# In the cross steps, the heads are normalised in front of row maximum 6

## The chip, the core and the metric

The kernel runs on one core of one Trainium2 chip. A core has five engines that run side by side, each through its own instructions in a fixed order: TensorE (PE, with its weight loads listed apart as PEld), VectorE (DVE), ScalarE (ACT), GpSimd (POOL) and SyncE (SP), which here only starts transfers. They wait for one another through semaphores. The metric is the time of one execution in device microseconds, as the median of several runs.

## What is computed

The reference is a decoder of two layers on 16 sequences of 256 tokens and 256 features. Layer 0 is windowed self attention, cross attention to a context of 77 tokens with a padding mask per sequence, and a mixture of 8 experts of which each token takes two. Layer 1 is causal self attention, cross attention with one mask for all sequences, and a quantised gated network. Cut to what matters here:

```python
x = x + window_attention(layernorm(x))            # call 1, items 0 to 15
x = x + cross_attention(layernorm(x), ctx, pad)   # call 1, items 16 to 31
x = x + mixture_of_experts(layernorm(x))
x = x + causal_attention(layernorm(x))            # call 2, items 0 to 15
x = x + cross_attention(layernorm(x), ctx, mask)  # call 2, items 16 to 31
x = x + gated_network(x)
# attention of one sequence, 16 heads of 16 features
scores = q @ k.T / 4 ; p = exp(scores - rowmax(scores)) ; heads = (p @ v) / rowsum(p)
```

## The kernel before

`attention` is called twice, once for each layer. In the trace the tiles of the first call carry the name window, those of the second the name causal, also where they work for the cross attention. A call handles 32 items: item 0 to 15 is the self attention of one sequence each, item 16 to 31 its cross attention. The work of one item is spread over several steps of a software pipeline. In step `ref`, item `ref` has its layernorm turned and its projections made, item `ref - 1` has its scores and row maxima, item `ref - 2` its shifted scores, exponentials and first products with the values, item `ref - 3` the last of these products and its heads, and item `ref - 4` its output projection. `active(ref, lag)` says whether there is such an item. In the last items of a call, statistics for what follows are added (`last_ln`), and in call 1 the choice of experts as well (`find_best` and `choose`, L1114 to L1138, from step 22 on).

Every engine has its own `step`, written out by hand as a loop over eight slots `i`, and this order is all that sets the order of its work. `wide(ref)` is true where the layer of item `ref - 2` handles two pairs of heads at once:

```python
GROUP = {"window": 1, "causal": 1, "cross_pad": 2, "cross_mask": 2}
def wide(ref):
    return active(ref, 2) and layer_at(ref, 2).pairs == 2
```

So the wide steps are the cross steps, 18 to 33 of each call; the others are the self steps.

The parts that the change and the prediction touch, for a wide step:

- TensorE, `wide_slot` (L2073): in slot 6 it makes `scores` 6 (L1685 for the padding, L1692), then `early_maxima` (L1849), then `heads_out` (L2009), which turns the heads of item `ref - 3` into the bank `psb` and raises `o_mm`, then `shifted` 6 (L1721, L1726). In slot 7 it makes `first_quads` (L1746) and then `turn_outputs` (L1831), which waits for `o_norm`. The next step begins with `scores` 0, `turn_normed` (L1831), `shifted` 0, then in slot 1 the first half of the query projection (L1877) and `late_maxima` (L1849), and in slot 2 `scores` 2.
- `scores` writes the two banks of `ps1`, which every call of it uses again, so it waits until VectorE has taken the row maxima before (`s1_max`). In a wide step it is called in slots 0, 2, 4 and 6.
- VectorE, `step` (L1256): `row_max` 6 waits for `scores` 6 and reduces `ps1`. With the padding mask that is one reduction (L1078), with the common mask it is eight masked ones (L1072, each followed by a read of its result). Behind it in slot 6 stands the normalisation of the heads: a wait for `o_mm`, a reciprocal (L1272), a wait for it, two multiplications (L1277), and `o_norm` is raised. Then follow in slots 6 and 7 the statistics of the rows just finished (L75, L80), `split_max` (L1053, L1055), which `late_maxima` waits for, `low_key` (L1036), and in call 1 the choice of experts; then the next step's `row_max` 0, for which `scores` 2 waits. In slot 4 VectorE waits for the output projection (`add_output`, L1090), in slot 5 of call 2 it takes a peak (L1292).
- SP copies queries and keys of item `ref` into `q_pair` and `k_pair` (L615, L622). It takes the keys first, after `k_lo` from `low_key` and after `shifted` 2.
- GpSimd takes the inverse deviation of the last statistics (L53, L55) and sends rows to the experts (L814).

In the self steps the same normalisation stands in slot 6 behind that slot's row maximum too, and a row maximum is taken in every one of the eight slots.

Of the kernel before, what the change touches and what calls it, by code (L numbers as in the profile page):

```python
# [12 lines left out]
ALU = mybir.AluOpType  # L13
# [6 lines left out]
H = 16  # L20
HD = D // H
P = 128
# [61 lines left out]
def normalise(nc, ln, par, rows, out, normed, b):  # L84

    for s in range(ST):
        op = nc.vector.tensor_scalar(out[:, s, :], rows(b, s), ln["mv"][par][:, s, 0:1],
                                     ln["rstd"][par][:, s:s + 1], ALU.subtract, ALU.mult)
    op.then_inc(normed, 1)
# [98 lines left out]
def attention(nc, layers_in, x_sb, q_pair, k_pair, v_aug, ident, selects, to_all, eye, parts, merge=None, tail=None, route=None,  # L188
# [8 lines left out]
    with ExitStack() as ctx:  # L197
        def sb(name, shape, dt):
            return ctx.enter_context(nc.sbuf_tensor(f"{tag}_{name}", shape, dt))
# [21 lines left out]
        recip = sb("recip", [P, ST * H], F32)  # L221
# [132 lines left out]
        o_mm = sem("o_mm")  # L354
        recip_done = sem("recip_done")
        o_norm = sem("o_norm")
# [52 lines left out]
        o_heads = psb[:, :, :].rearrange("p a (h d) -> p (a h) d", d=VW)  # L409
        o_by_half = o_tok[:].rearrange("p s (q a j) d -> p a (s q) j d", a=2, j=2)  # L410
# [44 lines left out]
        def active(ref, lag):  # L455

            return 0 <= ref - lag < N
# [5 lines left out]
        def wide(ref):  # L463

            return active(ref, 2) and layer_at(ref, 2).pairs == 2
# [45 lines left out]
        def layer_at(ref, lag=0):  # L511

            return layers_in[(ref - lag) // B]
# [16 lines left out]
        def in_x(t, ref):  # L530

            r = ref // B
            return lambda i, s: row_of(t - r * B, s)
# [17 lines left out]
        with nc.Block(no_gpsimd_drain=True) as block:  # L551
            @block.sync
            def _(sp):
# [26 lines left out]
                if load:  # L580
                    x_view, _, x_second, x_loaded = load
                    sp.dma_start(x_sb[:, ST:TILES // 4, :], x_view[:, ST:TILES // 4, :]).then_inc(x_second, 16)
# [396 lines left out]
            def _(dve):  # L979
# [78 lines left out]
                def row_max(t, ref, i):  # L1058

                    L = layer_at(ref, 1)  # L1060
                    if i % L.pairs:
                        return
                    hf, j = i // 4, i % 4
                    dve.wait_ge(s1_mm, before(t, ref, 1) + i // L.pairs + 1)
                    if L.mask_nat is not None:
                        gate(dve, dve_passed)
                        junk = 0
                        for p in range(L.pairs):
                            for qt, _, nk, col in L.direct:
                                for ab in range(2):  # L1070
                                    nk_real = min(nk, L.nk)
                                    op = nc.vector.tensor_tensor_reduce(  # L1072
                                        masked[:, junk:junk + nk_real], ps1[:, ab, p * L.width1 + col:p * L.width1 + col + nk_real],
                                        L.mask_nat[0][:, col:col + nk_real], 1.0, LEAST_SCORE, ALU.add, ALU.max,
                                        m_tok[:, hf, ab, j + p, qt:qt + 1])
                                    junk += nk_real
                    else:
                        op = nc.vector.reduce_max(  # L1078
                            m_tok[:, hf, :, j:j + 2, :].rearrange("p a j s -> p a (j s)"),
                            ps1[:, :, 0:2 * L.width1].rearrange("p a (j k) -> p a j k", j=2 * ST)[:, :, :, 0:S2], AX.X)  # L1080
                    op.then_inc(s1_max, 1)
# [165 lines left out]
                def next_rows(t, ref):  # L1247

                    if active(ref, -1):
                        par = (ref + 1) % 2  # L1250
                        dve.wait_ge(scaled_by, t + 2)
                        if ref >= 1:
                            dve.wait_ge(xT_mm, t)
                        normalise(nc, ln, par, in_x(t + 1, ref + 1), xn[par], normed, t + 1)

                def step(t, ref):  # L1256
                    par = ref % 2
                    if ref == B:
# [6 lines left out]
                    for i in range(PAIRS_H):  # L1265
                        if i == 4 and wide(ref):
                            next_rows(t, ref)
                        if active(ref, 1):
                            row_max(t, ref, i)
                        if i == 6 and active(ref, 3):  # L1270
                            dve.wait_ge(o_mm, t - 2)
                            nc.vector.reciprocal(recip[:].unsqueeze(2), o_heads[:, :, HD:HD + 1]).then_inc(recip_done, 1)  # L1272
                            dve.wait_ge(recip_done, t - 2)
                            for ab in range(2):
                                heads = slice(ab * H, ab * H + H)
                                by_quad = lambda x: x.rearrange("p (q j) d -> p q j d", j=2)
                                op = nc.vector.tensor_tensor(o_by_half[:, ab], by_quad(o_heads[:, heads, 0:HD]),  # L1277
                                                             by_quad(recip[:, heads].unsqueeze(2).to_broadcast([P, H, HD])), ALU.mult)
                            op.then_inc(o_norm, 1)
                        if i == (4 if wide(ref) else 1) and active(ref, 4):  # L1280
                            add_output(t, ref, 4)
                        late = bool(merge) and ref == 0
# [5 lines left out]
                        if i == (3 if ref == N + 3 else 5 if wide(ref) else 1) and tail and in_tail(ref, 5):  # L1288
# [3 lines left out]
                            op = nc.vector.tensor_reduce(tail.peak[:, bass.ds(e, 1)], last_xn[0], AX.XY, ALU.max,  # L1292
                                                         apply_absolute_value=True)
# [63 lines left out]
                if not merge:  # L1357
                    scale_layer(0)
                dve.wait_ge(loaded[0], 16 * n_load[0])
                steps(dve, step)  # L1360
                if route:
                    tile_table()
# [1674 lines left out]
```

## Time and profile before

| | |
|---|---|
| median of 3 runs | 2112.07 us (2107.06 to 2112.20) |
| the profiled execution | 2101.48 us, its span 2099.7 us |
| PE, PEld busy in the span | 1948.5 us (93%), 1597.3 us (76%) |
| DVE, ACT, POOL busy | 1233.8 us (59%), 979.4 us (47%), 686.7 us (33%) |
[...]

Times in the rows are microseconds from the start of the span. The trace is of one execution; the time of that execution is given beside its span, since some 1.8 us lie around it.

### The profile page before, as it was taken

How to read it: one execution, taken by the hardware profiler on the slowest of the kernel's cores; microseconds unless marked ns; L12 is line 12 of the kernel's file. 1: busy time of each engine (PE TensorE's matmuls, PEld its weight loads, DVE VectorE, ACT ScalarE, POOL GpSimd, SP SyncE). 2: the span in 40 equal slices, each digit the busy share in tenths (PEclk: the TensorE clock that was granted, in tenths of full speed). 3: DMA queues.
4: the chain of work that ended last, by engine and by line, in shares of the span. 5: the costliest groups of instructions: out<-in, count | busy, mean ns of one | idle time of the engine just before them, and what ended most of it. 6: DMA issues, size and time to landing. Idle time of an engine off the chain costs nothing. (4 is left out here: it accounts for less than half of the span.)

```text
span 2099.7 us, 57083 instructions
## 1 busy us (share of the span) xinstructions
PE 1948.5 (93%) x19802; PEld 1597.3 (76%) x19802; DVE 1233.8 (59%) x5200; ACT 979.4 (47%) x1905; POOL 686.7 (33%) x1244
## 2 busy tenths in 40 slices
PE   7999998999959999999999789999899998999889
PEld 5788886777749999999999578887677775444377
DVE  5788885676541111111115588998778886369964
ACT  2555555676613333333333255556566663357400
POOL 2666665256560000000001545553422220013400
PEclk8999999999969999999999999999999999999999
DMA  7333332334339999999995534433233330000023
GB/s 217 110 109 112 120 129 83 103 113 135 104 120 402 376 339 344 344 340 341 339 343 221 176 119 146 130 125 128 88 96 114 110 108 27 0 0 0 0 71 91
DMA packets 209555, 334.74 MB, mean 159 GB/s; under 512 B 59502, under 2 KB 193427, under 8 KB 200307
## 3 DMA queue, kind: packets, MB, share of 16 engines
q1 hardware_dynamic: 194914, 301.82, 41.6%
q0 software_dynamic: 9552, 26.10, 4.1%
q10 hardware_dynamic: 4928, 4.72, 0.7%
q8 instruction: 97, 1.59, 0.3%
q14 instruction: 64, 0.52, 0.1%
HBM read 193.74 MB, written 28.05 MB: 106 GB/s over the span
## 5 line engine op out<-in xcount | busy, mean ns | idle before, releaser
L2369 ACT ACTIVATE moe_h<-moe_h_ps,moe_weights 128x128 f32<-128x128 f32 x424 | 132.8, 364 | 255.5 <-PE moe_h_ps L2337 226.0
L2802 PE MATMUL ffn_prod_ps<-x_sb,ffn_weights 128*128 128x512 f32 x480 | 209.4, 596 | 7.0 <-ACT ffn_sig_q L2788 7.0
L2401 DVE TENSOR_TENSOR moe_y<-moe_y_ps,moe_weights 128x256 f32<-128x256 f32 x53 | 22.5, 425 | 328.1 <-PE moe_y_ps L2349 328.1
L2280 POOL DMA_DIRECT2D moe_y_dram<-moe_y x71 | 39.4, 555 | 491.4 <-DVE moe_y L2401 483.2
L1403 ACT ACTIVATE causal_prob<-causal_ps 128x768 f32<-128x768 f32 (+1 forms) x192 | 168.8, 879 | 63.0 <-PE causal_ps L1726 62.2
L2337 PE MATMUL moe_h_ps<-moe_h,moe_weights 128*128 128x128 f32 x1696 | 198.0, 275 | 0.0
L2337 PEld LDWEIGHTS moe_h_ps<-moe_h,moe_weights 128*128 128x128 f32 x1696 | 193.6, 192 | 0.1
L2802 PEld LDWEIGHTS ffn_prod_ps<-x_sb,ffn_weights 128*128 128x128 f32 x480 | 90.6, 191 | 123.6 <-issue 109.3
L1072 DVE CUSTOM_DVE_ANT_0 causal_masked<-causal_ps,causal_causal_mask 128x256 bf16<-128x256 f32 (+1 forms) x512 | 151.9, 353 | 28.6 <-PE causal_ps L1692 27.7
L1072 DVE CUSTOM_DVE_ANT_0 window_masked<-window_ps,window_window_mask 128x160 bf16<-128x160 f32 x512 | 135.1, 320 | 46.3 <-PE window_ps L1692 44.9
L1692 PE MATMUL causal_ps<-k_pair,q_pair 64*128 64x78 f32 (+2 forms) x1024 | 102.2, 299 | 20.5 <-DVE causal_m_tok L1072 9.3
L1692 PEld LDWEIGHTS causal_ps<-k_pair,q_pair 64*128 64x128 f32 x1024 | 77.5, 190 | 51.0 <-DVE causal_m_tok L1072 31.3
L2657 DVE TENSOR_REDUCE ffn_peak<-ffn_wide 128x1 f32<-128x1024 f32 x72 | 87.1, 1212 | 47.9 <-ACT ffn_wide L2762 47.9
L1692 PE MATMUL window_ps<-k_pair,q_pair 64*128 64x160 f32 (+1 forms) x1024 | 103.7, 302 | 9.8 <-DVE window_m_tok L1072 5.8
L1403 ACT ACTIVATE window_prob<-window_ps 128x640 f32<-128x640 f32 x128 | 90.0, 703 | 45.3 <-PE window_ps L1726 44.1
L2319 PE MATMUL moe_h_ps<-moe_rowsT,moe_weights 128*128 128x128 f32 x848 | 103.5, 275 | 1.0 <-DMA moe_weights<-moe_w_in 1.0
L1692 PEld LDWEIGHTS window_ps<-k_pair,q_pair 64*128 64x128 f32 x1024 | 78.8, 189 | 33.0 <-DVE window_m_tok L1072 19.9
L2349 PE MATMUL moe_y_ps<-moe_weights,moe_h 128*128 128x256 f32 x424 | 100.4, 380 | 0.7 <-ACT moe_h L2369 0.7
L2319 PEld LDWEIGHTS moe_h_ps<-moe_rowsT,moe_weights 128*128 128x128 f32 x848 | 98.9, 192 | 1.2 <-DMA moe_weights<-moe_w_in 1.2
L850 POOL TENSOR_SCALAR_AFFINE_SELECT causal_prob<-causal_prob 128x512 f32<-128x512 f32 x128 | 80.2, 651 | 59.0 <-ACT causal_prob L1403 58.8
L1072 DVE CUSTOM_DVE_ANT_0 causal_masked<-causal_ps,causal_cross_mask 128x77 bf16<-128x77 f32 x512 | 86.1, 235 | 16.1 <-PE causal_ps L1692 15.9
L1721 PE MATMUL window_ps<-window_m_rows,selects 64*128 64x320 f32 (+1 forms) x512 | 89.4, 375 | 6.3 <-ACT window_prob L1403 6.1
(424 smaller groups left out, 4753.4 us busy)
## 6 DMA issues: line engine op xcount, KB each, us to landing
moe_weights<-moe_w_in SPq DMA_DIRECT2D x53, 2180.0 KB, 9.8
q_pair<-parts SPq DMA_DIRECT2D x512, 128.0 KB
parts<-moe_w_in SPq DMA_DIRECT2D x17, 2180.0 KB, 9.1
k_pair<-parts SPq DMA_DIRECT2D x256, 128.0 KB
k_pair<-parts SPq DMA_DIRECT2D x256, 38.5 KB
moe_y_dram<-moe_y POOLq DMA_DIRECT2D x71, 128.0 KB, 4.0
moe_rows<-moe_slots_dram SPq DMA_DIRECT2D x53, 128.0 KB, 3.7
x_before_ffn_dram<-x_sb SPq DMA_DIRECT2D x16, 256.0 KB, 2.1
```

The source lines that it names most:

```text
L850: op = nc.gpsimd.affine_select(out=m, in_=m, compare_op=ALU.is_ge, fill=0.0, base=0, pattern=[[0, 4], [1, P]], channel_multiplier=-1)
L1072: op = nc.vector.tensor_tensor_reduce(masked[:, junk:junk + nk_real], ps1[:, ab, p * L.width1 + col:p * L.width1 + col + nk_real], L.mask_ ...
L1403: nc.scalar.activation(out, src, ACT.Exp).then_inc(expd, 1)
L1692: op = nc.tensor.matmul(ps1[:, ab, j * L.width1 + col:j * L.width1 + col + nk], q_pair[par][rows_of[ab], i + j, qt * P:qt * P + P], k_pair ...
L1721: nc.tensor.matmul(dst.rearrange("p (s t) -> p s t", s=tiles), L.selects[rows_of[ab], i % 4 + j, 0:kr], m, start=(fresh and j == 0 and n = ...
L2280: pool.dma_start(route.y_dram[bass.ds(j * TM, TM), :].rearrange("(s p) d -> p s d", p=P), y[r][:])\
L2319: op = nc.tensor.matmul(h1_ps[:, f // 2, (f % 2) * TM:(f % 2) * TM + TM], w1[:, k, f * P:f * P + P], rowsT[:, k, :], start=(k == 0), stop= ...
L2337: op = nc.tensor.matmul(h2_ps[:, f // 2, (f % 2) * TM:(f % 2) * TM + TM], w2[:, k, f * P:f * P + P], h1[:, k, :], start=(k == 0), stop=(k ...
L2349: op = nc.tensor.matmul(y_ps[:, r % YR, s * D:s * D + D], h2[:, k, s * P:s * P + P], w3[:, k, :], start=(k == 0), stop=(k == FB - 1))
L2369: nc.scalar.activation(out[:, f, :], psum[:, f // 2, (f % 2) * TM:(f % 2) * TM + TM], ACT.Gelu, bias=bias[:, f:f + 1]).then_inc(done, 1)
L2657: return nc.vector.tensor_reduce(out, rows, AX.XY, ALU.max, apply_absolute_value=True)
L2802: op = nc.tensor.matmul(prod_ps[:, slot, f, :].rearrange("p (b t) -> p b t", b=2), w[:, k, at:at + P], x_cols(n // GROUPS, k), start=(k == ...
```

## The change

The normalisation becomes a function, `normalise_heads`. In wide steps it is called in front of row maximum 6; in the other steps it stays behind it. The short description of the change speaks of self steps, but the test in the code is `wide(ref)`, which holds in the cross steps. No instruction is added or removed on any engine; on VectorE a wait, a reciprocal and two multiplications change places with one row maximum.

```diff
+                def normalise_heads(t):
+
+                    dve.wait_ge(o_mm, t - 2)
+                    nc.vector.reciprocal(recip[:].unsqueeze(2), o_heads[:, :, HD:HD + 1]).then_inc(recip_done, 1)
+                    dve.wait_ge(recip_done, t - 2)
+                    for ab in range(2):
+                        heads = slice(ab * H, ab * H + H)
+                        by_quad = lambda x: x.rearrange("p (q j) d -> p q j d", j=2)
+                        op = nc.vector.tensor_tensor(o_by_half[:, ab], by_quad(o_heads[:, heads, 0:HD]),
+                                                     by_quad(recip[:, heads].unsqueeze(2).to_broadcast([P, H, HD])), ALU.mult)
+                    op.then_inc(o_norm, 1)
...
+                        if i == 6 and active(ref, 3) and wide(ref):
+                            normalise_heads(t)
                         if active(ref, 1):
                             row_max(t, ref, i)
-                        if i == 6 and active(ref, 3):
-                            dve.wait_ge(o_mm, t - 2)
...
-                            op.then_inc(o_norm, 1)
+                        if i == 6 and active(ref, 3) and not wide(ref):
+                            normalise_heads(t)
```

## Rows read from the trace of the kernel before

**Rows 1.** Busy time by stretch: us, then each engine's, the clock, DMA.

```profile
core 0: us, PE busy (x) PEld busy (x) DVE busy (x) ACT busy (x) POOL busy (x), PEclk, DMA share, GB/s
419.00:566.00 147.00, 140.63 (x2054) 114.45 (x2052) 100.30 (x360) 100.59 (x181) 86.63 (x201) 1.00 0.40 122
1577.00:1725.00 148.00, 136.13 (x2004) 110.50 (x2006) 125.33 (x885) 90.50 (x158) 40.74 (x86) 1.00 0.36 110
```

**Rows 2.** Waits from 419 to 566: us in total, times, longest.

```profile
DVE x_sb L1090 <- PE window_psa L1877: 21.6, 10, 2.3
...
PE window_ps L1685 <- DVE window_m_tok L1078: 1.6, 8, 0.2
```

**Rows 3.** Timeline of DVE, step 24 into 25: start, duration, [idle before].

```profile
446.37 0.80 DVE L1078 TENSOR_REDUCE window_m_tok<-window_ps 128x8 f32<-128x616 f32 x1
447.35 0.36 DVE L1272 RECIPROCAL window_recip<-window_psb 128x32 f32<-128x32 f32 x1 [0.18 <-PE window_psb L2009]
447.74 0.76 DVE L1277 TENSOR_TENSOR window_o_tok<-window_psb,window_recip 128x256 f32<-128x256 f32 x2
448.41 0.74 DVE L75 BATCH_NORM_STATS2 window_last_stats<-x_sb 128x6 f32<-128x256 f32 x2
...
451.64 0.79 DVE L1078 TENSOR_REDUCE window_m_tok<-window_ps 128x8 f32<-128x616 f32 x1
452.35 0.74 DVE L75 BATCH_NORM_STATS2 window_stats<-x_sb 128x6 f32<-128x256 f32 x2
```

**Rows 4.** Timeline of PE over the same steps.

```profile
446.60 0.71 PE L2009 MATMUL window_psb<-ident,window_o_aug 64*128 64x64 f32 x16
...
448.73 0.46 PE L1831 MATMUL window_psb<-ident,window_o_tok 64*128 64x64 f32 x8
449.03 0.30 PE L1685 MATMUL window_ps<-window_pad_now,to_all 64*128 64x312 bf16 x2
...
452.49 0.30 PE L1685 MATMUL window_ps<-window_pad_now,to_all 64*128 64x312 bf16 x2 [0.21 <-DVE window_m_tok L1078]
```

**Rows 5.** Timeline of SP in step 25: the first copies of keys.

```profile
454.67 3.19 SPq L622 DMA_DIRECT2D k_pair<-parts  x4
```

**Rows 6.** Timelines of DVE and PE, steps 18 to 20.

```profile
363.06 0.17 DVE L1053 CAST window_m_cols<-window_m_tok 128x16 fp32r<-128x16 f32 x1
...
363.67 0.30 PE L1685 MATMUL window_ps<-window_pad_now,to_all 64*128 64x312 bf16 x2
...
384.15 0.31 PE L1685 MATMUL window_ps<-window_pad_now,to_all 64*128 64x312 bf16 x2 [0.82 <-DMA k_pair<-parts]
```

**Rows 7.** Timeline of PE, step 33 of call 1.

```profile
569.62 0.31 PE L1849 MATMUL window_psa<-ident,window_m_cols 64*72 64x64 f32 x4 [0.39 <-DVE window_m_cols L1055]
```

**Rows 8.** Timeline of DVE, call 2, a looped wide step into the next.

```profile
1620.08 0.68 DVE L1292 TENSOR_REDUCE x_peak<-causal_got 128x512 f32 x1
...
1621.93 0.35 DVE L1272 RECIPROCAL causal_recip<-causal_psb 128x32 f32<-128x32 f32 x1
...
1625.19 0.24 DVE L1072 CUSTOM_DVE_ANT_0 causal_masked<-causal_ps,causal_cross_mask 128x77 bf16<-128x77 f32 x1 [0.33 <-PE causal_ps L1692]
```

**Rows 9.** Timeline of PE over the same steps.

```profile
1620.68 0.70 PE L2009 MATMUL causal_psb<-ident,causal_o_aug 64*128 64x64 f32 x16
...
1624.10 0.46 PE L1831 MATMUL causal_psb<-ident,causal_o_tok 64*128 64x64 f32 x8
1624.37 0.62 PE L1692 MATMUL causal_ps<-k_pair,q_pair 64*128 64x78 f32 x8
...
1627.25 0.65 PE L1692 MATMUL causal_ps<-k_pair,q_pair 64*128 64x78 f32 x8
```

**Rows 10.** Timeline of PE, call 2, step 19 into 20.

```profile
1547.71 0.69 PE L2009 MATMUL causal_psb<-ident,causal_o_aug 64*128 64x64 f32 x16
...
1550.39 0.65 PE L1692 MATMUL causal_ps<-k_pair,q_pair 64*128 64x78 f32 x8
```

**Rows 11.** Timeline of PE, call 1, a self step: scores 7.

```profile
141.11 0.45 PE L1692 MATMUL window_ps<-k_pair,q_pair 64*128 64x160 f32 x4
```

More of the change, by code:

```diff
@@ L1267, in step @@
                             next_rows(t, ref)
+                        if i == 6 and active(ref, 3) and wide(ref):
+                            normalise_heads(t)
                         if active(ref, 1):
                             row_max(t, ref, i)
-                        if i == 6 and active(ref, 3):
-                            dve.wait_ge(o_mm, t - 2)
[L1272 to L1278, printed above, removed]
-                            op.then_inc(o_norm, 1)
+                        if i == 6 and active(ref, 3) and not wide(ref):
+                            normalise_heads(t)
                         if i == (4 if wide(ref) else 1) and active(ref, 4):
```

## The prediction

> **What bounds the kernel now.** I read the busy time by stretch first, to see which engine the wide steps lean on. In ten cross steps of call 1 (419 to 566 us) TensorE is busy for 140.63 of 147 us and VectorE for 100.30; in ten of call 2 TensorE has 136.13 of 148 and VectorE 125.33. [...] So TensorE hardly rests, and what makes it rest is what counts. The view of waits is next. In those steps of call 1 TensorE stood eight times at the first scores of a slot until a row maximum of VectorE was done, up to 0.2 us each [rows 2]. Then the timelines of both engines show which row maximum that is, and what VectorE did before. It is row maximum 0, which ends at 452.43; scores 2 start at 452.49 after an idle 0.21 us [rows 3, 4]. Follow VectorE back from there. Its work follows on without a wait from the reciprocal at 447.35, and that one waited for TensorE's turned heads, which end at 447.31 [rows 3, 4]. So there is a **ring**: TensorE turns the heads, VectorE normalises, does the statistics, the split of the maxima, the low key part, the choice of experts and row maximum 0, TensorE goes on with scores 2 and comes round to the next heads. Each side waits for the other once in a step. Row maximum 6 lies outside this ring today. It runs from 446.37 to 447.17, while TensorE is still turning heads, and VectorE idles for another 0.18 us behind it [rows 3].
>
> **The change part by part.** Nothing is added or removed: the wait, the reciprocal and two multiplications move in front of one row maximum. They issue no transfer and pass no queue but VectorE's own. What is queued behind the moved wait is row maximum 6, and behind that all of slots 6 and 7.
>
> *Can the heads come out sooner?* In call 1 no. The reciprocal already starts 0.04 us after the heads are there, whatever stands in front of it [rows 3, 4]. TensorE takes the normalised heads at 448.73, straight from other work, while they are ready at 448.50 [rows 3, 4]. The moved part gains nothing there.
>
> *Steps 22 to 32 of call 1, with the choice of experts.* The normalisation keeps its time, from 447.35 to the start of the next operation at 448.41. Row maximum 6 then takes that place. Start to start, such a reduction holds VectorE for 0.71 us (451.64 to 452.35 [rows 3]). All that follows is later by 0.71, row maximum 0 included, and as TensorE waits for it already, scores 2 start 0.71 later. Scores 0 of the step have to wait as well, but only 0.25 us (below), and this is part of the same 0.71. The next heads are late by as much, so that nothing of it is won back and the next step adds its own. VectorE's large idle time, 21.6 us in ten waits for the output projection [rows 2], lies behind scores 2 and doesn't help. In step 32 no scores follow; there TensorE waits in the next step for the split maxima [rows 7], which are late by the same 0.71. 11 steps times 0.71 are 7.8 us.
>
> *Steps 18 to 21 of call 1.* There is no choice of experts, so VectorE has time before row maximum 0. What remains is scores 0, which write where row maximum 6 reads. Row maximum 6 would start at 363.06, where the split starts now, and end 0.80 later at 363.86; with 0.06 us to TensorE, as between 452.43 and 452.49, scores 0 start at 363.92 in place of 363.67 [rows 3, 4, 6]. That is 0.25 in each of four steps, 1.0 in all. In one of them TensorE waits 0.82 us for a copy of keys soon after [rows 6], which swallows part. I take 0.7, between 0.5 and 1.0.
>
> *Call 2, looped steps 21 to 30.* Row maximum 6 is longer here. It starts at about 1620.68, when the peak reduction of 0.68 us is nearly done, and the reciprocal follows at 1621.93, so it holds VectorE for about 1.26 us; the heads are there at 1621.38 [rows 8, 9]. After the change VectorE waits for them, starts the reciprocal at 1621.42, the row maximum 1.06 later at 1622.48, and ends it at about 1623.8. Scores 0 start at 1624.37 [rows 9], so they don't notice. What follows is later by 0.74, of which 0.33 is idle time in front of row maximum 0 today [rows 8]. It ends 0.41 later, at about 1627.0, and scores 2 start at 1627.25 [rows 9]. The cost is nothing, covered by TensorE's own work; with a cover 0.25 thinner it would show. The normalised heads come 0.5 earlier, but TensorE takes them at 1624.10, a microsecond after they are ready at 1623.0 [rows 8, 9], so that is worth nothing either.
>
> *Call 2, the other steps.* In steps 18 to 20 there is no wait for statistics in between, and TensorE comes to scores 0 sooner after the heads. The heads end at 1548.40; 0.04 for the signal, 1.06 for the normalisation, some 1.34 for the row maximum (its 1.26 and the 0.08 by which an operation outlasts the start of the next) and 0.06 back give 1550.90, and scores 0 start at 1550.39 now [rows 3, 10]: 0.51 each, 1.5 in three steps. Copies of keys swallow a part as above. The last step can lose up to 0.7 as in call 1. I take 1.5 for all, between 0.5 and 2.2.
>
> *Other queues.* SP's first keys of a step wait for the low key part, which ends near 450.3 and would end near 451.0; SP starts them at 454.67, behind shifted scores [rows 5], so they don't move. GpSimd's scaling of the last rows and the sending to the experts follow VectorE, late by the same 0.71 as TensorE itself.
>
> **Sum.** 7.8 + 0.7 + 1.5 = 10.0 us. The profiled execution took 2101.48 us, so it would take 2111.5. The median of the runs is 2112.07, or 10.6 above it; to that I add the same 10.0: 2122. With the bounds of the terms it is 8.8 to 11.0, and if each step's 0.71 were instead the gap that TensorE has now to its scores 0, 0.25, it would be 11 times 0.25, 0.7 and 1.5, or 5.0. Runs of one kernel lie 5 us apart, so 0.3%, or 6.3 us, is about what a measurement can tell from no change.
>
> **The rivals.**
>
> *No cost to see (2112 to 2117).* VectorE is idle for 46.7 us of the 147, 4.7 in each step, against 0.71 to be hidden [rows 1]. If the late row maxima were caught up before TensorE comes to them, nothing or only the 0.25 at scores 0 would remain: 0 to 5.0 us. [...] Against it: the idle time is not where the ring needs it, and each step of [rows 4] already has a wait of 0.21 at the very instruction that would be late. I give it 0.20.
>
> *Faster (2104).* In call 2 the heads are normalised 0.5 us earlier in each step. If TensorE's turning of the outputs were what that step waits for, 15 steps would give 7.5 us back. It decides from where the normalised heads arrive later than TensorE's products before them end; today they arrive 1.0 us earlier [rows 8, 9]. And the ring of call 1 would have to cost nothing as well, or the two cancel. 0.05.
>
> *The change does what its short description says.* Were the self steps meant and changed, the 1.06 us of normalisation would stand in front of a row maximum behind which scores 7 start at once, at 141.11 [rows 11], in 30 steps: about 32 us, 2144. The test `wide(ref)` in the diff excludes it, as it holds where two pairs are handled at once, which only the cross layers do. 0.02.
>
> **How the numbers follow.** The forecast, the ring, has 0.73, and I predict its time, 2122. The range of 2112 to 2129 takes in its bounds with the spread between runs, and most of the first rival; the other two are left out. Of the forecast 0.03 may read as no change, as its 10 us are not far above 6.3. So faster has 0.05, within 0.3% has 0.20 + 0.03 = 0.23, slower has 0.70 + 0.02 = 0.72.
>
> **What would show it.** In the changed profile, steps 22 to 30 of call 1 should take 0.71 us longer each; the wait of TensorE for row maximum 0 at scores 2 should grow from 0.2 to about 0.67 (0.21 + 0.71 - 0.25), and one of about 0.25 should appear at scores 0. The reciprocal should start as soon after the heads as now, with a wait of about 0.9 before it. The looped steps of call 2 should not grow. If TensorE's waits at scores 2 stay at 0.2, the ring is not the bound; if the turning of outputs starts sooner, the second rival is right; if self steps change, the third is.

## The result, and the profile after

The changed kernel takes 2116.05 us as the median of 21 runs, the kernel before 2106.73 us in 21 runs beside them: a ratio of 1.0041, with a 95% interval of 1.0028 to 1.0054. By this ratio it is slower by 8.6 us, between 5.9 and 11.4; the two medians lie 9.3 us apart. The prediction said slower by 10.0, and 2122.0 as the time. The profiled execution took 2114.78 us, its span 2113.0, where the one before had 2101.48 and 2099.7.

Read first how long a step is. The reciprocal of the heads comes once in each step. These are those of step 22 and of step 32 of call 1 in the changed kernel:

```profile
417.70 0.36 DVE L1259 RECIPROCAL window_recip<-window_psb 128x32 f32<-128x32 f32 x1 [1.23 <-PE window_psb L2015]
...
574.10 0.36 DVE L1259 RECIPROCAL window_recip<-window_psb 128x32 f32<-128x32 f32 x1 [0.95 <-PE window_psb L2015]
```

Ten steps take 156.40 us; before they took 149.28. All ten grew alike, by 0.65 to 0.75 us: nine of them from about 15.0 to 15.7 us, the last, which is shorter, from 14.25 to 15.00. Taking such starts for each part of a call gives a table in which only the place of the change differs (the last two columns are experiments told below):

| reciprocal to reciprocal, us | before | changed | call 1 only | call 2 only |
|---|---|---|---|---|
| call 1, steps 18 to 22 | 55.42 | 54.89 | 54.68 | 54.74 |
| call 1, steps 22 to 32 | 149.28 | 156.40 | 156.48 | 149.25 |
| call 1, steps 32 to 34 | 20.69 | 21.54 | 21.06 | 20.26 |
| call 2, steps 18 to 22 | 57.18 | 57.64 | 57.00 | 57.08 |
| call 2, steps 22 to 31 | 133.11 | 133.17 | 133.12 | 132.96 |
| the rest of the span | 1684.0 | 1689.4 | 1697.0 | 1686.0 |

The five parts together grow by 7.96 us. But for the end of call 2, which comes below, the rest of the span has the same order of work in all four kernels, and it still spreads over 13 us. That is why single executions say little here and the steps say much.

Now the waits. The view of waits of the changed kernel over the ten steps (engine, line, releaser, us in total, times, longest) answers to [rows 2]:

```profile
PE window_ps L1691 <- DVE window_m_tok L1078: 8.5, 10, 0.9
...
DVE x_sb L1090 <- PE window_psa L1883: 21.6, 10, 2.3
...
DVE window_recip L1259 <- PE window_psb L2015: 8.2, 9, 1.0
```

TensorE's wait for a row maximum was 1.6 us in all and is now 8.5. VectorE has a new wait of 0.9 in front of each reciprocal. Its long wait for the output projection is what it was: 21.6 us of idle time that help nobody.

The busy time by stretch, in the same columns as [rows 1], says the same in another way:

```profile
419.30:573.40 154.10, 140.73 (x2054) 114.28 (x2051) 100.71 (x361) 101.73 (x181) 86.90 (x201) 1.00 0.38 117
```

It holds the same work as the first stretch of [rows 1] (2054 products both times) in 7.1 us more. TensorE's 140.73 busy us, VectorE's 100.71 and the granted clock of 1.00 are those of before. All of the loss is waiting.

VectorE's timeline, steps 24 into 25, answers to [rows 3]:

```profile
449.06 0.36 DVE L1259 RECIPROCAL window_recip<-window_psb 128x32 f32<-128x32 f32 x1 [0.91 <-PE window_psb L2015]
449.46 0.76 DVE L1264 TENSOR_TENSOR window_o_tok<-window_psb,window_recip 128x256 f32<-128x256 f32 x2
450.13 0.79 DVE L1078 TENSOR_REDUCE window_m_tok<-window_ps 128x8 f32<-128x616 f32 x1
450.84 0.74 DVE L75 BATCH_NORM_STATS2 window_last_stats<-x_sb 128x6 f32<-128x256 f32 x2
...
454.07 0.79 DVE L1078 TENSOR_REDUCE window_m_tok<-window_ps 128x8 f32<-128x616 f32 x1
```

Row maximum 6 now stands between the products and the statistics and holds VectorE from 450.13 to 450.84, which is 0.71 us. Row maximum 0 starts 5.01 us behind the reciprocal, where it was 4.29 [rows 3].

TensorE's timeline over the same steps answers to [rows 4]; L2015 turns the heads, L1837 the outputs and then the normalised rows:

```profile
448.31 0.72 PE L2015 MATMUL window_psb<-ident,window_o_aug 64*128 64x64 f32 x16
...
449.44 1.07 PE L1752 MATMUL window_psa<-window_prob,v_aug 77*32 77x256 f32 x16
450.44 0.46 PE L1837 MATMUL window_psb<-ident,window_o_tok 64*128 64x64 f32 x8
451.02 0.31 PE L1691 MATMUL window_ps<-window_pad_now,to_all 64*128 64x312 bf16 x2
...
451.51 0.48 PE L1837 MATMUL window_psa<-ident,window_xn 64*128 64x64 f32 x8
...
454.92 0.31 PE L1691 MATMUL window_ps<-window_pad_now,to_all 64*128 64x312 bf16 x2 [0.90 <-DVE window_m_tok L1078]
```

The heads end at 449.03 and the reciprocal starts 0.03 later: as soon as before. Scores 0 start 1.99 us behind the heads, where it was 1.72 [rows 4]; 0.16 of these 0.27 us show as an overlap with the turning of the outputs that is gone (449.03 to 449.19 [rows 4]), not as idle time. Scores 2 (454.92) wait 0.90 us.

In the loop of call 2 nothing moves. TensorE's timeline there answers to [rows 9]:

```profile
1602.60 0.70 PE L2015 MATMUL causal_psb<-ident,causal_o_aug 64*128 64x64 f32 x16
...
1606.30 0.62 PE L1698 MATMUL causal_ps<-k_pair,q_pair 64*128 64x78 f32 x8
...
1609.18 0.65 PE L1698 MATMUL causal_ps<-k_pair,q_pair 64*128 64x78 f32 x8
```

Scores 0 and 2 come 3.00 and 5.88 us behind the end of the heads, before 2.99 and 5.87 [rows 9]. In the steps in front of the loop TensorE does wait at scores 0, as forecast:

```profile
1562.18 0.64 PE L1698 MATMUL causal_ps<-k_pair,q_pair 64*128 64x78 f32 x8 [0.52 <-DVE causal_m_tok L1072]
```

### The profile page after: what moved, and what is told of

Its sections match the earlier page's. It is cut to its first block and busy times, and to the rows that moved or that the text cites. A ratio compares the mean times of both kernels' runs of the same rounds, so it can differ in the third digit from the quotient of the medians.

```text
span 2113.0 us, 57083 instructions
## 1 busy us (share of the span) xinstructions
PE 1956.3 (93%) x19802; PEld 1602.3 (76%) x19802; DVE 1236.7 (59%) x5200; ACT 981.5 (46%) x1905; POOL 689.2 (33%) x1244
```

## The experiments

**Where the loss is made.** The normalisation goes in front in one call alone (`route` holds in call 1).

```diff
-                        if i == 6 and active(ref, 3) and wide(ref):
+                        if i == 6 and active(ref, 3) and wide(ref) and route:
```

The second kernel has `not route` there. In both, the call behind the row maximum takes the other steps.

> The normalisation stands in front of row maximum 6 in the cross steps of call 1 alone; call 2 is as before. The ring theory (VectorE's chain from the heads to row maximum 0 sets the step, and the row maximum now stands in it): ten steps from the reciprocal of step 22 to that of step 32 take 156.4 us as in the changed kernel, against 149.3 before, and TensorE waits 0.9 us at scores 2 of each; the whole is 7 to 8 us over the kernel before. The rival that the delay is covered and the measured loss is made in call 2 or elsewhere: ten steps of 149.3, and a total within 2 us of the kernel before.

> The normalisation stands in front of row maximum 6 in the cross steps of call 2 alone; call 1 is as before. The ring theory: the ten steps of call 1 take 149.3 us, the looped steps of call 2 keep 14.8 us each, three steps before the loop show a wait of TensorE of about 0.5 us at scores 0, and the whole is 0 to 2 us over the kernel before. The rival that call 2 gains from the earlier normalisation: its looped steps become shorter, and the whole is up to 7 us under the kernel before. The rival that the loss is made in call 2: 7 to 9 us over it.

Call 1 only: 2113.23 us, 1.0037 (1.0023 to 1.0050) of the kernel before, and ten steps of 156.48. Call 2 only: 2105.40 us, 1.0005 (0.9987 to 1.0023), ten steps of 149.25, three waits of 0.5 us at scores 0 and a loop that is as long as before. So the loss is made in call 1, 7.1 us of it in steps 22 to 32. That call 2 gains 7.5 us from the earlier normalisation is excluded.

**The same reduction put in front of the heads and behind them.** Both kernels take row maximum 6 twice in steps 22 to 32, the first time into a spare tile.

```diff
+                        if i == 6 and inline(ref, 6):
+                            nc.vector.reduce_max(
+                                spare[:, (ref - 22) * 8:(ref - 21) * 8],
+                                ps1[:, :, 0:2 * L.width1].rearrange("p a (j k) -> p a j k", j=2 * ST)[:, :, :, 0:S2], AX.X)
```

> The kernel before, but in steps 22 to 32 of call 1 row maximum 6 is taken twice, the first time into a spare tile (work that the reference does not need), in front of the normalisation. The ring theory: of the extra 0.71 us the first 0.18 to 0.26 fall into VectorE's idle time in front of the reciprocal, the rest delays the ring, so each step grows by 0.45 to 0.53 us and ten steps take 153.8 to 154.6 us in place of 149.3. The rival that VectorE's idle time covers it: 149.3. The rival that a reduction costs its whole length wherever it stands: 156.4.

> The changed kernel with the same extra reduction, which now stands behind the normalisation, in front of row maximum 6. The ring theory: there is no idle time left in the chain, so each step grows by the whole 0.71 us, to 16.4, and ten steps take 163.5 us in place of 156.4. The rival that the change has brought the steps to another bound, with room in VectorE: 156.4.

Each of these two kernels ran once, in 2106.90 and 2139.44 us, so only the steps can be compared. With the order of before, nine steps take 15.39 to 15.44 us, and ten 153.39: 0.41 more each, a little under the 0.45 expected. With the changed order eight steps in a row take 16.37 to 16.56, 0.71 more each. So 0.71 us of VectorE cost 0.41 at a place with free time behind it, and all of it where there is none. How much is free is better read from start to start than from the idle 0.18 us. In the first of the two kernels the reciprocal follows row maximum 6 without a gap, 0.70 us from start to start:

```profile
447.49 0.79 DVE L1083 TENSOR_REDUCE window_m_tok<-window_ps 128x8 f32<-128x616 f32 x1
448.19 0.35 DVE L1277 RECIPROCAL window_recip<-window_psb 128x32 f32<-128x32 f32 x1
```

In the kernel before it was 0.98 (446.37 to 447.35 [rows 3]), so 0.28 us were free, and 0.71 less 0.28 is 0.43. The view of waits of the first kernel shows that it comes out at scores 2 again, and that TensorE now also waits for the normalised heads:

```profile
PE window_ps L1690 <- DVE window_m_tok L1083: 5.3, 10, 0.6
...
PE window_psb L1836 <- DVE window_o_tok L1282: 2.5, 9, 0.3
```

The last two of the ten steps of the second took 17.21 and 20.98 us, so the whole ten took 169.5, not 163.5. That is not VectorE, which is busy for 18.51 of the last 38.20 us. The busy time by stretch, first eight steps and then the rest up to step 32 (us, then PE, PEld, DVE, ACT, POOL, clock, DMA, GB/s), shows the clock:

```profile
422.00:553.32 131.32, 115.10 (x1700) 93.46 (x1698) 90.76 (x312) 84.61 (x152) 71.46 (x168) 1.00 0.37 112
553.32:591.52 38.20, 35.17 (x400) 28.08 (x398) 18.51 (x62) 18.68 (x30) 15.18 (x34) 0.78 0.28 88
```

**The ring made shorter.** If the chain to row maximum 0 sets the step, taking something else out of it must give the loss back. The choice of experts takes 1.44 us there (452.63 to 454.07 in the changed kernel). It is moved behind row maximum 0 of the next step, and GpSimd's `note` behind that step's layer norm:

```diff
+        def deferred(ref):
+
+            return inline(ref, 6) and wide(ref) and wide(ref + 1)
...
+                        if i == 1 and deferred(ref - 1):
+                            find_best(t - 1, ref - 1)
+                            choose(t - 1, ref - 1)
```

> The kernel before, with the choice of experts taken out of the ring: in steps 22 to 32 VectorE does it one slot later, behind row maximum 0 of the next step, and GpSimd notes it there too. The ring theory: row maximum 0 comes about 1.4 us earlier, TensorE's wait of 0.2 us at scores 2 is gone, and ten steps take about 147 us in place of 149.3, 2 us in all. The rival that TensorE's own work is what sets the step: the wait goes and comes back at another place, 149 us or more. The rival that the later choice makes the ranks or GpSimd's layer norm late: a new wait of TensorE in slot 2, or steps above 15.0 us.

> The changed kernel with the same deferred choice of experts. The ring theory: the 1.4 us taken out of VectorE's chain are more than the 0.71 us that the row maximum put in, so TensorE's 0.9 us at scores 2 is gone and ten steps take what they take in the kernel before with the deferred choice, within 0.5 us; the change then costs 0 to 1 us in call 1. The rival that the change costs by making row maximum 6 itself late for scores 0: its ten steps stay some 7 us longer than those of the kernel before with the deferred choice.

With the order of before: 2102.12 us, 0.9981 (0.9969 to 0.9993); ten steps of 145.92, and no wait at scores 2 is left. The gain is 3.4 us where 2 were expected, since the choice's 1.4 us took away a lost overlap as well as the idle 0.2: scores 2 now start 0.11 us behind the start of the turned maxima (450.04 to 450.15), where it was 0.52 (451.97 to 452.49). VectorE's timeline shows the new order, the low key part followed at once by row maximum 0, and the choice behind the statistics:

```profile
447.86 0.50 DVE L1042 SCALAR_TENSOR_TENSOR parts<-window_cross_pad_k_now,window_cross_pad_bk,parts 128x77 fp32r<-128x77 f32 x2
448.28 0.79 DVE L1084 TENSOR_REDUCE window_m_tok<-window_ps 128x8 f32<-128x616 f32 x1
...
450.04 0.26 DVE L1125 TENSOR_TENSOR window_gates<-window_seen_at,window_gate_b 128x16 f32<-128x16 f32 x1
```

With the changed order the expectation missed: 2109.96 us, 1.0021 (1.0008 to 1.0034), and ten steps of 151.99, 6.1 more than with the order of before. The waits at scores 2 are gone there too. Two things took their place. Six of the ten steps take 14.84 to 15.18, some 0.2 to 0.55 more than 14.63. TensorE's turning of the last rows (L1846) is late, because it needs the low part of the queries, and VectorE, without any idle time since the reciprocal at 435.71 but 0.15 us behind each of two statistics, starts that at 444.40:

```profile
444.40 0.86 DVE L1042 SCALAR_TENSOR_TENSOR parts<-window_psb,window_cross_pad_bq,parts 128x256 fp32r<-128x256 f32 x2
```

```profile
444.81 0.64 PE L1707 MATMUL window_ps<-k_pair,q_pair 64*128 64x78 f32 x8
445.47 0.46 PE L1846 MATMUL window_psb<-ident,ffn_weights 64*128 64x64 f32 x8
```

The turning starts 0.66 us behind scores 4; with the order of before it was 0.46 (439.87 to 440.33). The ring has a second, longer end. And two steps took 16.5 us without any longer wait: the clock fell. The busy time by stretch through one of them, in the columns as above:

```profile
459.40:460.40 1.00, 0.94 (x20) 0.62 (x13) 1.00 (x3) 1.00 (x2) 0.51 (x2) 1.00 0.33 75
...
460.60:463.60 3.00, 3.00 (x27) 2.74 (x26) 0.92 (x2) 2.14 (x4) 2.14 (x3) 0.50 0.54 169
```

The clock is 0.50 over these 3 us. TensorE had been busy for 0.94 of the microsecond from 459.40 to 460.40, with the clock at 1.00.

**Is the fall of the clock chance, and is the second end real?** One kernel repeats the deferred choice with the change in call 1 alone. Two others make the low part of the queries ahead of the split of slot 3, one in each order:

```diff
+                        if i == 3 and active(ref, 0) and deferred(ref - 1):
+                            low_part(q_parts[par], q_ps, layer_at(ref).bq, q_hi, q_lo, t, S)
                         if i == 3 and active(ref, 1):
                             split_max(t, ref, 1, 0)
```

> The deferred choice again, with the normalisation in front in the cross steps of call 1 alone; call 2 is as before. In the kernel with the deferred choice and the whole change, eight of ten steps took 14.9 to 15.2 us, and two took 16.5, in which the granted clock stood at 0.50 for some 3 us. If those falls of the clock were chance, ten steps take 148.5 to 150 us; if this order of work brings them about, there are such steps again and ten take 151 us or more. Against the kernel before with the deferred choice (145.9) at least 2.3 us remain by either, as TensorE waits 0.23 us in each step for the low part of the queries, which is now behind the late row maximum and the choice in VectorE.

> The changed kernel with the deferred choice and one more edit: in the steps with a deferred choice VectorE makes the low part of the queries in front of the split of the maxima of slot 3, 1.07 us earlier. If the remaining loss of the changed kernel with the deferred choice is the end of one VectorE chain, the wait of 0.23 us in front of TensorE's turning of the last rows goes, and steps without a fall of the clock take 14.6 to 14.7 us like those of the kernel before with the deferred choice. If the falls of the clock hung on that wait, there are none, and ten steps take 146 to 147 us; if they hang on something else in this order of work, some steps still take 1.6 us more. The rival that the change costs something beside this chain: steps of 14.85 us remain.

> The kernel before with the deferred choice and the low part of the queries in front of that split. TensorE did not wait for that part there, so nothing is left to win: ten steps take 145.9 us as without the second edit, and the total is within 2 us of it, some 3 to 4 us under the kernel before. If the split of the maxima, now 0.86 us later, were waited for, the steps would grow.

The change in call 1 alone: 2109.30 us, 1.0015 (1.0002 to 1.0028), ten steps of 150.16, one of them 16.49 with the clock at 0.50. That lies between the two expectations and decides neither. With the low part first and the changed order: 2104.42 us, 0.9988 (0.9971 to 1.0006), six of ten steps at 14.64 to 14.66, four at 14.78 to 14.83, and no step of 16.5. With the low part first and the order of before: 2102.90 us, 0.9979 (0.9963 to 0.9996), ten steps of 145.79, as expected no gain over the deferred choice alone. TensorE's rows of the changed order confirm the second end; the turning (L1848) follows 0.47 us behind scores 4 again:

```profile
447.14 0.64 PE L1709 MATMUL window_ps<-k_pair,q_pair 64*128 64x78 f32 x8
447.61 0.46 PE L1848 MATMUL window_psb<-ident,ffn_weights 64*128 64x64 f32 x8
```

The ten steps take 147.1 us against 145.8. Of the 7.1 us that the change costs there, 1.3 are left once VectorE's chain has been made shorter at two places. Of these, 0.95 lie in the last of the ten steps alone (14.82 us against 13.87), and the first nine differ by 0.36. In step 32 TensorE has no query projection to make, so it comes sooner to the turning of the split maxima (L1866), and VectorE still splits them behind the late row maximum 6. The view of waits of the changed order shows it:

```profile
PE window_psa L1866 <- DVE window_m_cols L1061: 0.7, 1, 0.7
```

**The self steps too.** The normalisation stands in front of row maximum 6 in every step: the test on `wide(ref)` is left out.

> The normalisation stands in front of row maximum 6 in the self steps as well, what the short description of the change would be if it were meant word for word. The third rival of the prediction: 1.06 us more in each of 30 self steps, as scores 7 follow at once behind row maximum 6, so some 28 to 32 us over the changed kernel. The rival that other work covers it: the self steps stay at 18.3 us in call 1 and 19.5 in call 2.

2165.20 us, 1.0282 (1.0251 to 1.0313): 49 us over the changed kernel, not 28 to 32. Most self steps of call 1 grow from about 18.2 to 20.8 us; the first eight of call 2 grow from about 19.5 to between 20.7 and 21.8. TensorE's timeline of a self step shows scores 7:

```profile
107.20 0.45 PE L1696 MATMUL window_ps<-k_pair,q_pair 64*128 64x160 f32 x4 [1.66 <-DVE window_m_tok L1072]
```

The wait is 1.66 us and not 1.06, as VectorE first waits for the heads and then does the normalisation and the row maximum. The rest goes with the clock, which the stretches around that wait show:

```profile
105.20:107.20 2.00, 0.34 (x10) 0.19 (x6) 1.91 (x11) 0.97 (x2) 1.84 (x4) 1.00 0.46 154
107.20:108.60 1.40, 1.40 (x26) 1.29 (x30) 0.75 (x7) 0.53 (x1) 0.14 (x1) 0.93 0.00 0
108.60:111.60 3.00, 3.00 (x42) 2.36 (x34) 2.26 (x11) 1.37 (x3) 2.44 (x4) 0.50 0.31 95
```

TensorE is busy for 0.34 of 2 us, then takes up work at 107.20, and from 108.60 to 111.60 the clock is 0.50. Call 2 lets the two parts be told apart. TensorE waits at a row maximum for 1.6 us in each of the two steps below, but the clock falls only in the second:

```profile
1329.46:1350.28 20.82, 18.54 (x250) 15.54 (x250) 17.95 (x87) 11.59 (x21) 10.95 (x16) 1.00 0.41 126
...
1371.01:1392.63 21.62, 19.79 (x250) 16.77 (x250) 17.97 (x86) 11.70 (x21) 11.12 (x17) 0.92 0.39 123
```

The changed kernel takes 19.5 us for either. So the wait alone costs 1.3 us there, and the fall of the clock 0.8 more.

## Why the prediction was right

*The ring.* Right, in kind and size. The ten steps from 22 to 32 grew by 0.71 us each in the mean, the whole length of the reduction. The kernels with twice the reduction (0.41 in front, 0.71 behind) and with a shorter chain (7.1 us of loss down to 1.3, most of it at the split of the same late row maximum) show that it is the chain on VectorE; where the remaining 0.36 us of nine steps come from was not looked into. That nothing is won back is shown as well, as each step adds its own. The eleventh, step 32, ends in a step without a row maximum 6, so it is taken from the turning of the heads (L2015) to the next one: 12.20 to 12.21 us in six kernels with the change in call 1, 11.49 to 11.65 in four without it (without the two with twice the reduction). That is 0.7, and the eleven steps cost 7.1 + 0.7 = 7.8 us, as forecast.

*Heads as soon as before, and nothing from the earlier normalisation.* Right: 0.03 us from heads to reciprocal, and the turning of the outputs follows the products directly, in both calls.

*Scores 0 in steps 18 to 21.* This term was mis-sized: 0.7 us forecast, no loss measured (54.7 to 55.0 us from step 18 to 22 in the seven kernels with the change in call 1, 54.7 to 56.1 in the five without it, where waits for copies of keys as in [rows 6] make the difference). The 0.27 us at scores 0 are there, and so is the step that the forecast left out: the next thing that TensorE does is turn the normalised rows (L1837), and it may not until ScalarE has copied the first products out of the bank. ScalarE's row, before and then changed:

```profile
448.95 0.58 ACT L1475 ACTIVATE window_o_aug<-window_psa 128x512 f32<-128x512 f32 x1
```

```profile
450.67 0.58 ACT L1481 ACTIVATE window_o_aug<-window_psa 128x512 f32<-128x512 f32 x1
```

The copy ends at 449.53 and 451.25; the turning starts at 449.79 and at 451.51, 0.26 us behind it both times. Scores 0 had that much room. For the same reason the wait at scores 2 is 0.90 and not 0.67: the delay at scores 0 is not carried on to scores 2, so all of the 0.71 adds to the 0.21. The period was not touched by this, as 0.71 is the sum either way.

*Call 2.* The loop is unchanged, as forecast. In steps 18 to 22 the copies of keys scatter the times; six kernels with the change take 57.1 to 58.5 us there, six without it 55.8 to 57.2, and the means are 1.3 apart. The last step, which the forecast had at up to 0.7, loses 0.4 to 0.5: from the turning of the heads in step 32 to the next one the six kernels with the change take 11.81 to 11.90 us, the six without it 11.40 to 11.43. The kernel with the change in call 2 alone shows the wait for the split maxima there:

```profile
1743.05 0.36 PE L1855 MATMUL causal_psa<-ident,causal_m_cols 64*85 64x64 f32 x4 [0.24 <-DVE causal_m_cols L1055]
```

Together that is 1.7 us (forecast 1.5, bounds 0.5 to 2.2).

*The sum.* 7.8 + 0 + 1.7 = 9.5 us by the steps, 8.6 (5.9 to 11.4) by the runs, 10.0 forecast. The time itself is 6 us under the forecast, nearly all because the median before is 2106.73 in 21 runs, not the 2112.07 of the first three.

*The rivals.* No cost to see: it rested on VectorE's idle time, and the 21.6 us behind scores 2 stayed as idle as they were; it was true in call 2, where it covers the loop. Faster: nothing of it in the loop. The self steps: not this change, and the price of that rival was too low, 49 us over the changed kernel where the self steps were put at 32, since the wait is longer and the clock falls.

## What to carry to other kernels

Ask of a moved instruction what it stood beside and what it stands in front of now. Row maximum 6 was free while TensorE was turning heads and cost its whole length once it stood behind a wait for them, on an engine that is busy for 100.71 of 154.10 us. When a wait passes round two engines once in a step, look for work that can leave the ring: with the choice of experts moved out of it, the kernel beats both, at 0.9981 (0.9969 to 0.9993) of the kernel before. And when one end of a chain is relieved, look for the instruction that is late next; here it was the low part of the queries, 0.2 us behind.

## What was not expected

The granted clock. It fell to 0.50 for stretches such as that from 460.60 to 463.60 above; there it had a mean of 0.86 from 463.60 to 464.50 and 1.00 from 464.50 to 468.00. In the self steps of the last experiment each step of call 1 has a mean clock of 0.83 to 0.92, where the changed kernel has 1.00 in the first thirteen of the fifteen. These steps grew by more than the wait in them: most by about 2.6 us, with a wait of 1.66 at scores 7. The clock also fell without a wait of that length. In three of twenty steps with the deferred choice and the changed order the clock fell although TensorE had been busy without a pause longer than 0.3 us, and each such step took 1.6 us more; in the ten steps of the other kernels, the changed one with twice the reduction apart, it did not. Why these steps and no others was not settled: the falls went with the late turning of the last rows, but one kernel without them is no proof. The clock also falls in stretches that all kernels share: from the reciprocal of step 17 of call 1 to the next one its mean is 0.77 to 0.84 in all twelve. And it does not fall at the same places in each trace: in steps 32 to 34 of call 1 its mean is 0.96 in the changed kernel and 1.00 with the change in call 1 alone. That may be one reason why executions of one program lie several microseconds apart: of the 21 runs of the changed kernel, the three with a mean clock of 0.969 took 2116.94 to 2126.25 us, the three with 0.975 or more 2108.32 to 2112.99. That the clock is the cause was not shown.
